# SyncE fetches two of every 104 tiles of gathered rows, one row per DMA, in the two conv passes, and one in the last pass

## What is computed

```python
# two convolutions (L = 0, 1)
e   = relu(edge_weight @ W_l0 + b_l0) @ W_l1 + b_l1
msg = relu(x[src] + e)                       # a row of 96 floats for every edge
agg = segment_sum(msg, dst, num_segments=N)
h   = relu(relu((x + agg) @ WL0 + bL0) @ WL1 + bL1)
# then a message layer with batch statistics
message = relu(concat([x[row], x[col], edge_feat]) @ W_msg + b_msg)
agg     = segment_sum(normalised(message), col)
out     = layernorm(x + agg + node_feat)
```

## Time and profile before

| | |
|---|---|
| median of the three timed runs | 12210.97 us |
| span of the profiled execution | 14691.4 us |
| TensorE (PE) busy | 9543.3 us, 65% |
| VectorE (DVE) busy | 7533.7 us, 51% |
| ScalarE (ACT) busy | 4925.7 us, 34% |
| GpSimd (POOL) busy | 9148.4 us, 62% |

### The profile page before, as it was taken

One profiled execution on the slowest core, in us unless ns is written; L12 is line 12 of the kernel. 1 busy time (PEld: TensorE's weight loads), 2 busy tenths in 40 slices (PEclk: granted clock), 3 DMA queues, 4 the chain that ended last, 5 costly groups with the idle time before them and its releaser, 6 DMA issues. The chain is left out here.

```text
span 14691.4 us, 164775 instructions
## 1 busy us (share of the span) xinstructions
PE 9543.3 (65%) x34164; PEld 6790.2 (46%) x34164; DVE 7533.7 (51%) x15604; ACT 4925.7 (34%) x11020; POOL 9148.4 (62%) x9725
## 2 busy tenths in 40 slices
PE   3666666666666677777777777766555555555556
PEld 2544444444444444455555555544444444444444
DVE  3433434334333444455555555556666666666666
ACT  2322222222222333333333333333333333333333
POOL 6466666666666566666666666656666666666665
PEclk9999999999999655555555555555555555555555
DMA  3111111111111211122222222211122222212122
GB/s 80 32 40 40 40 41 40 41 40 40 41 40 40 54 42 43 43 47 45 46 46 46 47 46 45 47 43 41 42 45 43 44 43 44 44 44 44 43 44 47
DMA packets 580837, 647.55 MB, mean 44 GB/s; under 512 B 411208, under 2 KB 411689, under 8 KB 579722
## 3 DMA queue, kind: packets, MB, share of 16 engines
q0 software_dynamic: 309504, 476.02, 15.5%
q1 hardware_dynamic: 219142, 139.69, 3.9%
q10 hardware_dynamic: 51712, 27.54, 0.7%
HBM read 604.68 MB, written 39.43 MB: 44 GB/s over the span
## 5 line engine op out<-in xcount | busy, mean ns | idle before, releaser
L1309 PE MATMUL ps_pre<-w_e,conv_hid 97*128 97x96 f32 x12896 | 3268.4, 433 | 2144.1 <-DVE conv_part L600 1554.4
L1309 PEld LDWEIGHTS ps_pre<-w_e,conv_hid 97*128 97x128 f32 x12896 | 2873.9, 326 | 2886.6 <-issue 2393.8
L1309 PE MATMUL ps_pre<-last_w_q,last_hid 128*128 128x96 f32 x6448 | 1627.8, 432 | 1540.8 <-issue 935.3
L1309 PEld LDWEIGHTS ps_pre<-last_w_q,last_hid 128*128 128x128 f32 x6448 | 1440.1, 327 | 1928.3 <-issue 1605.6
L264 POOL DMA_INDIRECT early_got<-in_x_rows,early_idx x1612 | 1524.3, 946 | 960.5 <-issue 439.0
L264 POOL DMA_INDIRECT early_got<-h_rows,early_idx x1612 | 1520.8, 943 | 944.2 <-issue 478.3
L264 POOL DMA_INDIRECT early_got<-p_rows,early_idx x1612 | 1520.4, 943 | 926.6 <-issue 463.3
L264 POOL DMA_INDIRECT last_got<-p_rows,early_idx x1612 | 1520.8, 943 | 905.0 <-issue 430.5
L264 POOL DMA_INDIRECT conv_got<-h_rows,early_idx x1612 | 1520.8, 943 | 884.0 <-issue 435.6
L264 POOL DMA_INDIRECT conv_got<-in_x_rows,early_idx x1612 | 1520.7, 943 | 853.1 <-issue 447.1
L582 ACT ACTIVATE conv_part<-ps_pre 128x384 bf16<-128x384 f32 x1736 | 816.0, 470 | 3676.9 <-DVE ps_pre L641 2405.4
(11 more groups left out here) (255 smaller groups left out, 10572.7 us busy)
## 6 DMA issues: line engine op xcount, KB each, us to landing
conv_row<-ea_parts SPq DMA_DIRECT2D x372, 84.5 KB
last_row<-ea_parts SPq DMA_DIRECT2D x372, 84.5 KB
early_got<-in_x_rows,early_idx POOLq DMA_INDIRECT x1612
conv_got<-in_x_rows,early_idx POOLq DMA_INDIRECT x1612
early_got<-h_rows,early_idx POOLq DMA_INDIRECT x1612
conv_got<-h_rows,early_idx POOLq DMA_INDIRECT x1612
early_got<-p_rows,early_idx POOLq DMA_INDIRECT x1612
last_got<-p_rows,early_idx POOLq DMA_INDIRECT x1612
```

Source lines behind the costliest of these rows:

```text
L1309: mm = pe.matmul(ps["pre"][q % 2][:, t * C:(t + 1) * C], hid[q % 2][0:P if last else C1, t * P:(t + 1) * P], w_q[j % U][:, c * C:(c + 1) * ...
```

## The change

Tile 15 of slab 3 (`HAND[0]`) and tile 15 of slab 2 (`HAND[1]`) of every iteration are no longer gathered by POOL. SP fetches them, each row by a DMA of its own. `HAND_OF` says how many of the two a pass takes this way: both in `conv0` and `conv1`, the first alone in `last`. The third entry of a `HAND` tuple says in which slab's turn of SP's stream which rows are fetched: slab 3's tile in the turns of slabs 1, 2 and 3 (16, 64 and 48 rows), slab 2's in those of slabs 0 and 1 (72 and 56 rows).

The indices of such a tile are brought once more, as 128 numbers in one partition (`load_hand`). `fetch_rows` loads eight of them at a time into SP's registers and issues a DMA of one row of 384 bytes for each. It stands at the end of a slab's turn, behind `slab_rows`. POOL issues the other tiles (`pool_tiles`), and VectorE waits for `hand0` or `hand1` before it adds the chunk.

```diff
+BATCH = 8
+HAND = [(V - 1, 15, ((1, 0, 16), (2, 16, 80), (3, 80, 128))), (V - 2, 15, ((0, 0, 72), (1, 72, 128)))]
+HAND_OF = {"conv0": 2, "conv1": 2, "last": 1}
+def hand_rows(tiles, j):
+    return [(HAND[h], h, lo, hi) for h in range(tiles) for at, lo, hi in HAND[h][2] if at == j]
...
+def pool_tiles(tiles, j, g):
+    by_hand = [t for slab, t, _ in HAND[:tiles] if slab == j]
+    return [t for t in range(*group_tiles(g)) if t not in by_hand]
...
+                def load_hand(sp, h, k):
+                    slab, t, _ = HAND[h]
+                    sp.dma_start(hand_i[h][:].rearrange("o (p i) -> o p i", i=1),
+                                 a["src_t"][bass.ds(k * V + slab, 1), :, t:t + 1],
+                                 allow_slow_non_contiguous=True).then_inc(s[f"hand_idx{h}"], 16)
+                def fetch_rows(sp, k, j, final):
+                    for (slab, t, _), h, lo, hi in hand_rows(HANDS, j):
+                        sp.wait_ge(s[f"hand_idx{h}"], 16 * (k + 1))
+                        sp.nop(nofuse=True)
+                        if not opening(k):
+                            sp.wait_ge(s["add"], Q * (k - 1) + NC_ * slab + t // CH + 1)
+                        sp.nop(nofuse=True)
+                        for at in range(lo, hi, BATCH):
+                            _, nodes = nc.values_load_multi_w_load_instructions(
+                                hand_i[h][0:1, at:at + BATCH], engines=(mybir.EngineType.SP,), min_val=0, max_val=NPAD - 1,
...
+                            for p, node in zip(range(at, at + BATCH), nodes):
+                                sp.dma_start(got[slab][p:p + 1, t * C:(t + 1) * C], table[bass.ds(node, 1), :]).then_inc(s[f"hand{h}"], 16)
+                        if hi == P and not final:
+                            load_hand(sp, h, k + 1)
...
                             next_idx(k, j, final)
                             slab_rows(k, j)
+                            fetch_rows(sp, k, j, final)
...
-                                for i, t in enumerate(range(*group_tiles(g))):
+                                for i, t in enumerate(pool_tiles(HANDS, j, g)):
                                     if near:
                                         close(k, NC_ * j + g, i)
                                     gather(gp, table, got[j], idx[j], t, s[f"got{j}{g}"])
...
+                        for h, (slab, t, _) in enumerate(HAND[:HANDS]):
+                            if (slab, t // CH) == (j, c):
+                                v.wait_ge(s[f"hand{h}"], 16 * P * (k + 1))
                         add_gathered(v, j, q, q % 2, Q * k + q)
```

More of the change, by code:

```diff
@@ L205, in gnn_kernel @@
         fits = sb("fits", [1, 1], I32)
+        hand_i = [sb(f"hand_i{h}", [1, P], I32) for h in range(len(HAND))]
         ident = sb("ident", [P, P])
@@ L417, in edge_pass @@
             M = C1 if last else C
+            HANDS = HAND_OF[name]
             with ExitStack() as st:
@@ L533, in load_idx @@
                     load_slab_idx(sp, idx[j], slab, s[f"idx{j}"])
+                def load_hand(sp, h, k):
[13 more added lines that the diff above has]
+                                hand_i[h][0:1, at:at + BATCH], engines=(mybir.EngineType.SP,), min_val=0, max_val=NPAD - 1,
+                                skip_runtime_bounds_check_because="src names rows of the table, and the padding its last one")
+                            for p, node in zip(range(at, at + BATCH), nodes):
+                                sp.dma_start(got[slab][p:p + 1, t * C:(t + 1) * C], table[bass.ds(node, 1), :]).then_inc(s[f"hand{h}"], 16)
+                        if hi == P and not final:
+                            load_hand(sp, h, k + 1)
                 w_hid = w_hid1 if last else w_hid0_at if stats else w_hid0
@@ L1159, in landed @@
                         for g in range(len(GROUPS)):
-                            t0, t1 = group_tiles(g)
-                            sp.wait_ge(s[f"got{j}{g}"], 16 * (t1 - t0) * k)
+                            sp.wait_ge(s[f"got{j}{g}"], 16 * len(pool_tiles(HANDS, j, g)) * k)
                             sp.nop(nofuse=True)
@@ L1196, in sync_windows @@
                             load_idx(sp, j, j)
+                    for h in range(HANDS):
+                        load_hand(sp, h, 0)
                     def body(k, late, final=False):
@@ L1393, in add_rows @@
                             if c == start:
-                                t0, t1 = group_tiles(g)
-                                v.wait_ge(s[f"got{j}{g}"], 16 * (t1 - t0) * (k + 1))
+                                v.wait_ge(s[f"got{j}{g}"], 16 * len(pool_tiles(HANDS, j, g)) * (k + 1))
+                        for h, (slab, t, _) in enumerate(HAND[:HANDS]):
+                            if (slab, t // CH) == (j, c):
+                                v.wait_ge(s[f"hand{h}"], 16 * P * (k + 1))
                         add_gathered(v, j, q, q % 2, Q * k + q)
```

## The result

The changed kernel took 13,700.0 us (median of four runs, 13,696.6 to 13,701.5) beside 12,211.4 us for the kernel before (four runs): a ratio of 1.1218, 95% interval 1.1202 to 1.1234. It is slower, as forecast, and inside the range, but by 1489 us where 3029 were forecast.

A forecast was written before the change was run, and what follows sets the result against it. POOL's gathers were taken to bound the kernel before, and SP's instructions the conv passes after the change: 12,211 + 3069 (conv passes) − 39 (last pass) = 15,240 us, range 13,050 to 15,900.

The forecast's parts named there:

- POOL's step and the bound: POOL's gathers, 1.249 us each, bind the kernel before; 155 fewer give 194 us less, at best 12,017 us.
- One row, 0.41 us: SP's address computation, register move and single-row DMA take 0.41 us per row, bounds 0.294 and 0.50.
- The register load, 32 × 1.88 = 60 us: SP's loads of eight registers take 1.88 us each, 32 of them 60 us per conv iteration.
- The old work of SP, 12.5 us and 1 for the indices: SP's existing instructions take 12.5 us per conv iteration, and two new index loads 1 us.
- R3: Rival: dearer rows on SP, 0.50 us instead of 0.41, giving 16,640 us; chance 0.05.
- SP runs through, and the iteration takes SP's time: In conv passes SP never waits; its 179 us per iteration exceed POOL's 129.9 by 49.5, adding 3069 us.
- The last pass, −39 us: In last, SP's 116 us stay below POOL's 128.7, so the full gain of 39 us comes through.
- The rule of about 200 ns per register: The skill page's price for SP's register loads: 256 registers cost 51 us, not 60; total about 14,700.
- The cost of recording: Recording causes some 2440 us of POOL pauses in the profile before; the changed kernel's span would exceed 18,000 us.
- R1: Rival: SP binds, but its instructions are cheaper unrecorded, 145 us per iteration, +897, giving 13,110 us; chance 0.18.
- R2: Rival: POOL's gain comes through, 12,017 us, needing 0.445 us per SP row with its load share; chance 0.12.
- R4: Rival: no change, POOL's gain and SP's excess meeting, with SP at 129 to 130 us; chance 0.03.

The follow-up runs named there:

- shifted kernel: The changed kernel with the same 128 indices 4 bytes further into their buffer, each load starting there; 16,095.0 us, ratio 1.3173 to the kernel before.
- POOL's part alone: The changed kernel with nobody fetching the tiles POOL leaves out after each pass's first iteration, old rows added instead; 12,033.2 us, ratio 0.9853 to the kernel before.
- The kernel before repeated: The kernel before, unchanged, profiled once more on a different chip; 14,874 us in timed runs, profiled span 14,875.8 us.
- kernel with few loads: The changed kernel with registers loaded once per run of rows, the same eight rows fetched again, all 256 row DMAs kept; 12,065.2 us, ratio 0.9878 to the kernel before.

## Why the prediction was off

The numbers of this section are for a chip without stops, unless it says otherwise.

**POOL's step and the bound: right.** 1.249 us per gather, 127.4 us with 102 tiles, 128.7 with 103; leaving them out alone gave 179 us.

**One row, 0.41 us: right.** From one row to the next without a load between them it is 0.411 us in the median (counted in the trace). Over an iteration of conv0 L570 takes 72.5 us in DMAs, 19.5 in address computations and 16.7 in moves, gaps included: 108.7 us, where 105 were reckoned.

**The register load, 32 × 1.88 = 60 us: this is the step that failed.** It took 25.9 us per iteration. "This price is narrow" was wrong: the price had been extended from the seven-register load of L1188 to eight as if only the number counted. The shifted kernel shows that the place in memory counts for more than twice. The trace of before held the warning. L1188 starts at a different place in each of the four slabs' turns, and the one in four that starts on a multiple of 16 bytes from the buffer's start is a third cheaper: medians of 1.10 us in slab 0's turn and 1.63 to 1.64 in the other three (counted in the trace). One of these and the next one off the boundary, in the trace of before:

```profile
L1188 SPq TENSOR_LOAD <-head_i x1: 1110/1110/1110, 9917.0 to 9917.0; - x1
...
L1188 SPq TENSOR_LOAD <-head_i x1: 1655/1655/1655, 9950.1 to 9950.1; - x1
```

The median, 1634, with its maximum of 1655 beside it was read as one price with no scatter, and the minimum, 16, wasn't asked about. A quarter of the rows stood at 1.1 us.

**The old work of SP, 12.5 us and 1 for the indices: too low by 5.** It is 18.7 us (153.3 less 134.6). 2.6 to 3.3 us of it stand once per iteration between the branch at the loop's end and the next instruction. With a loop body of some 100 to 200 recorded SP instructions (POOL's part alone) it was 0.24 us; with 490 to 930 (the other four profiles without stops) it was 2.4 to 3.3. The prediction named the tenfold longer loop body under R3 and had no row for its price. That the code's length is the cause is a reading of these profiles.

**SP runs through, and the iteration takes SP's time: right.** TensorE's waits for `conv_row` and VectorE's 473 us for the rows are where the prediction put them.

**The last pass, −39 us: right, but by luck with the load.** Its period is 128.7. The prediction reckoned the tight place within the iteration with its dear load and took the full gain all the same. The shifted kernel has that dear load, 1.93 us, and there the period is 133.5 us: by the prediction's own price the last pass would have come near +110 us (31 × 3.6), inside the 5 us per iteration that it had kept for its upper end.

The sum with these sizes: 153.3 − 129.9 = 23.4 us per conv iteration, not 49.5, so 12,211 + 62 × 23.4 − 39 = 13,623. The 77 us to 13,700 lie mostly in the first iterations of conv0, whose first three take 185.5, 147.0 and 218.1 us, 94 above three median ones; why isn't known. So the load was priced 34 us per iteration too high, the rows and the rest 9 too low. With the load alone put right the forecast would have been about 13,110; part of its error was made good by the other one. Two sums of the prediction are also a little off: its parts, 105 + 60 + 1 + 12.5, are 48.6 us above POOL's 129.9 and not 49.5 (some 50 us in the total), and the terms of its upper end add up to 15,814, not 15,900.

**The rule of about 200 ns per register** (the Trainium skill, Runtime: NRT & Kernel Launch, section Instruction fetch mechanics). Its 14,700 us came nearer, but for no reason that the runs bear out: in loads of eight a register cost 98 ns on the boundary and 241 off it, and the measurement decides.

**The cost of recording: wrong.** The kernel before repeated shows it. Reckoning against 12,211 was right only because the result came from a chip like the one of those runs. The further claim, a span above 18,000 us from recording, fails with it: 13,699. The steps that the prediction took as undisturbed, 0.30 us between gathers and 0.18 around a DMA, held all the same.

**The rivals.** R1 (13,110) was near in number and wrong in kind: nothing of what stands between the records fell away. R2 fell: it needed 0.445 us per row, and a row with its share of the load costs 0.53 (134.6 / 256). For R2 the prediction named a sentence that the sequencer's part of a DMA is usually small relative to the DMA (the Trainium skill, DMA: Bandwidth & Descriptors, section Issuing engines are not separate DMA queues), and said that the trace doesn't bear it out for 384 bytes. That was too much: no row has the landing of a one-row DMA, and where landings show, as for the index loads of L276 (0.365 us to issue, 1.7 us to land), the trace agrees with the sentence. What decides here is another thing: transfers overlap, issues of one queue don't. In the kernel with few loads the 256 transfers cost next to nothing beside SP's time, and in the changed kernel SP's time is the bound. R3 fell as a price, 0.42 us per row and not 0.50. The "1.4 us stops of single SP instructions" that it named are real on chips with stops, and there they make the periods 212.7 and 218.4 us, but they lengthen the kernel before as well. R4 needed SP at 129 to 130 us; it is at 153.

## What to carry to other kernels

Before a queue is given many small instructions, multiply them out against the period that bounds the kernel: 256 rows at 0.425 us and 32 loads at 0.81 are 135 us, and that alone overfills a 127 us iteration, whatever the bytes. When a price is taken from a row, look at the spread behind its median and at what differs between the cheap and the dear ones, since it may be just what the new code does otherwise. And when a profile's span doesn't agree with the timed runs, find out which of the two the kernel will meet: a change that adds instructions to a queue can gain 0.9% on one chip and lose 10.6% on the next.

## What the runs showed of the hardware

**Register loads.** Loads of 32-bit values on SP took, by number and place: eight on a 16-byte boundary 0.78 us, eight 4 bytes past one 1.93, seven on one 1.11, seven off it 1.65, sixteen on it 1.14 to 1.23 (on chips with stops). Off the boundary this fits 0.1 us and 0.22 to 0.23 for each value. It made no difference whether such a load started 4, 8 or 12 bytes past a boundary, 1.63 to 1.64 us for seven in the kernel before, so it is where the load starts that counts, and not whether a boundary comes further on in it. On the boundary no one price for four values fits seven, eight and sixteen; the expectation that had one, 0.35 to 0.40, gave 1.5 to 1.7 us for sixteen and was too high.

**Stops of 0.7 us between instructions.** They go with the comparison and not with the kernel: none where the kernel before takes 12,211 us, hundreds in its own profile and thousands in that of the changed kernel where it takes 14,690 to 14,880. Each comparison ran on another chip, four with stops and one known one without, so the chip is the likely cause; that it isn't the hour wasn't tested, since no chip was used twice. They strike any kind of SP's instructions, at much the same places in each iteration. Set beside the profile without stops, instruction by instruction from the loop's branch on, an iteration of conv0 of the changed kernel (916 recorded instructions of SP, 25 iterations) loses 61 us, and 59 of it in four stretches: instructions 12 to 151, 311 to 403, 563 to 641 and 782 to 853, with nearly nothing between them; in conv1 it is much the same (counted in the traces). So the cost isn't in proportion to the instructions: from 256 to 192 rows the conv periods fell by 27 to 31 us, where 64 rows without stops are 34 us. A cause that goes by the place in the program would fit this. What makes the stops wasn't found, and no run tests it. POOL pauses as well on such a chip, 2 to 2.5 us at a time.
